# AdaLN block with attention and a mixture of experts: the down product with its operands exchanged, its sum moved to GpSimd, and another order of the three passes

## The reference

```python
h = _layernorm(x) * (1 + ca) + sa
x = x + ga * attention(h)                # 2 query heads of 128, one key and one value head, RoPE, causal
h = _layernorm(x) * (1 + cb) + sb
x = x + gb * ffn(h)

# ffn: 8 experts, all of them on every token, combined with a token's gate w[t, e]
gate = softmax(x @ Wg + bg); thr = sigmoid(x @ Wt + bt) * 0.125
w = (gate - thr) * (gate - thr >= 0);  w = w / sum(w)
h = gelu(x @ W1[e] + b1[e])              # 256 -> 1024
eo = h @ W2[e] + b2[e]                   # 1024 -> 256
out[t] = sum over e of w[t, e] * eo[e, t]
```

## Time and profile before

| | us |
|---|---|
| median of 3 runs | 1946.36 (1943.92 to 1947.73) |
| profiled execution | 1949.09 |
| its span, first to last instruction | 1947.3 |
| PE busy in the span | 1807.6 (93%) |
| DVE, ACT, POOL busy | 1304.9, 1048.1, 756.0 |
| mean granted TensorE clock | 0.968 |

### The profile page before, as it was taken

One profiled execution on the slowest core, in us unless ns is written; L12 is line 12 of the kernel. 1 busy time (PEld: TensorE's weight loads), 2 busy tenths in 40 slices (PEclk: granted clock), 3 DMA queues, 4 the chain that ended last, 5 costly groups with the idle time before them and its releaser, 6 DMA issues.

```text
span 1947.3 us, 32671 instructions
## 1 busy us (share of the span) xinstructions
PE 1807.6 (93%) x11616; PEld 1627.2 (84%) x11616; DVE 1304.9 (67%) x2472; ACT 1048.1 (54%) x2072; POOL 756.0 (39%) x1163
## 2 busy tenths in 40 slices
PE   5789947899589999999999999999999999999997
PEld 4679845798578999999999998888999999999996
DVE  3778747787666666666666666768666666666666
ACT  2567634676454555555555555554555555555553
POOL 4332124333364351615335161739244260624403
PEclk7999968999899999999999999999999999999998
DMA  4000000000000100101010010112110010101002
GB/s 112 26 15 23 18 11 17 23 18 9 31 23 23 33 23 22 42 4 44 11 34 31 14 44 1 33 33 89 53 33 22 23 34 12 44 12 33 12 1 65
DMA packets 56434, 56.04 MB, mean 29 GB/s; under 512 B 8384, under 2 KB 54480, under 8 KB 56272
## 3 DMA queue, kind: packets, MB, share of 16 engines
q1 hardware_dynamic: 56272, 53.95, 9.1%
HBM read 45.55 MB, written 8.39 MB: 28 GB/s over the span
## 4 chain that ended last, share of the span: by engine, by line
PE 62%; issue 5%; DVE 2%; ACT 2%; POOL 1%; POOLq 0%; DVEq 0%; ACTq 0%
PE score_ps L1075 10%; PE score_ps L1076 10%; PE score_ps L1077 9%; PE tr_ps L1110 5%; PE tr_ps L1108 5%; PE tr_ps L1106 5%; PE m_ps L1110 3%; PE m_ps L1108 3%; PE m_ps L1106 3%; PE o_ps L1108 3%; PE o_ps L1110 3%; PE o_ps L1106 3%; DVE h_lo L1276 1%; ACT h_hi L1209 1%; POOL h2f L1437 0%
## 5 line engine op out<-in xcount | busy, mean ns | idle before, releaser
L1205 ACT ACTIVATE g_sb<-c_sb,b_cols 128x512 f32<-128x512 f32 x384 | 276.0, 719 | 439.3 <-DVE c_sb L1340 288.1
L1276 DVE TENSOR_TENSOR h_lo<-g_sb,h_hi 128x512 fp32r<-128x512 f32 x512 | 398.6, 800 | 105.0 <-ACT h_hi L1209 105.0
L1075 PE MATMUL score_ps<-t_hi,w_hi 128*128 128x512 f32 x896 | 361.3, 403 | 27.6 <-ACT p_u L1235 12.2
L1076 PE MATMUL score_ps<-t_lo,w_hi 128*128 128x512 f32 x896 | 355.8, 397 | 0.0
L1077 PE MATMUL score_ps<-t_hi,w_lo 128*128 128x512 f32 x896 | 350.8, 392 | 0.0
L326 POOL TENSOR_TENSOR w_sums<-w_raw 128x128 f32<-128x128 f32 x64 | 42.7, 667 | 664.1 <-PE m_ps L1110 663.3
L1108 PE MATMUL tr_ps<-w_both,h_hi 128*128 128x256 f32 x1024 | 290.6, 284 | 0.0
L1110 PE MATMUL tr_ps<-w_both,h_lo 128*128 128x256 f32 x1024 | 290.5, 284 | 0.0
L1106 PE MATMUL tr_ps<-w_both,h_hi 128*128 128x256 f32 x1024 | 289.3, 283 | 0.0
L1209 ACT ACTIVATE h_hi<-c_sb,b_cols 128x512 fp32r<-128x512 f32 x384 | 271.6, 707 | 0.0
L1075 PEld LDWEIGHTS score_ps<-t_hi,w_hi 128*128 128x128 f32 x896 | 170.9, 191 | 54.5 <-ACT p_u L1235 12.2
(11 more groups left out here) (191 smaller groups left out, 4377.5 us busy)
## 6 DMA issues: line engine op xcount, KB each, us to landing
w_raw<-w_dram SPq DMA_DIRECT2D x128, 256.0 KB, 3.2
x_sb<-x_dram SPq DMA_DIRECT2D x32, 128.0 KB, 2.3
x_scratch<-x_sb SPq DMA_DIRECT2D x32, 128.0 KB, 1.7
t_sums<-x_scratch SPq DMA_DIRECT2D x8, 512.0 KB, 4.6
out_dram<-h2f SPq DMA_DIRECT2D x7, 512.0 KB, 3.2
probs_even<-wmod_dram SPq DMA_DIRECT2D x4, 256.0 KB, 3.9
probs_even<-wmod_dram SPq DMA_DIRECT2D x4, 128.0 KB, 2.3
probs_odd<-wqkvT_dram SPq DMA_DIRECT2D x1, 512.0 KB, 5.8
```

What stands on the lines that cost most here:

```text
L1075: nc.tensor.matmul(bank, hi, t_hi[p][:, b_, :], start=start, stop=False, skip_group_check=True)
L1076: nc.tensor.matmul(bank, hi, t_lo[p][:, b_, :], start=False, stop=False, skip_group_check=True)
L1205: nc.scalar.activation(g_sb[:, m % 2, :], source, ACT.Gelu_apprx_tanh, bias=bias).then_inc(act_g, 1)
L1276: nc.vector.tensor_tensor(h_lo[:, m % 6, :], g_sb[:, m % 2, :], h_hi[:, m % 6, :].bitcast(F32), ALU.subtract).then_inc(dve_lo, 1)
```

## The change

1. `down` exchanges its operands: a 128 x 128 block of W2 is stationary, the hidden values stream, 512 tokens at a time. The result has features on partitions and tokens along the bank. 2 feature halves x 3 passes per block, 24 passes of 512 per group.
2. In `product` and in `down` the passes come in the order low weights x high data, high x high, high weights x low data.
3. The gate is now needed along the free dimension, on all partitions. At the end of each batch's attention SP writes the gates, transposed, to DRAM (16 DMAs), and for each pair of an expert loads 1024 gates to all partitions (`g_rows`). b2 is loaded with features on partitions (`b2_cols`).
4. `evict` replaces `add`: four steps of 128 x 512, `(y + b2) * gate`, into the accumulator for expert 0, into `y_sb` otherwise. POOL then adds `y_sb` to the accumulator, two steps of 128 x 1024 per pair (not for the last pair). All bias work of PE, ACT and POOL goes.
5. The sums are turned back by PE, 16 turns of four 128 x 128 transposes in groups 72 to 79 and 121 to 128, scaled by DVE from PSUM (`scaled`, into `o_sb`) and added to x1 by POOL. The very last pair is turned from `y_sb` after its eviction and added to what the turns of the pair's earlier experts left.
6. `SLOTS` 5 to 4, the ring of `h_hi`, `h_lo` 6 to 5 (`RING`). `cast_tokens` moves ahead of the first GELU of a group, right behind the p_u copy. The low parts of the token sums move from POOL to DVE.

```diff
@@ constants
-SLOTS = 5
+SLOTS = 4
+RING = 5
@@ attention block, sync, after the tiles of batch b
+                    for half in range(NT // GT):
+                        sp.wait_ge(*done(dve_G2, b, "G2", half, 0, G2_STEPS))
+                        for t in range(half * GT, (half + 1) * GT):
+                            sp.dma_start(gT_dram[b, :, t * P:(t + 1) * P].rearrange("e p -> p e"),
+                                         gates[:, b * NT + t, :], allow_slow_non_contiguous=True).then_inc(s_gT[b], 16)
@@ experts, sync
+                    sp.dma_start(b2_cols[:], b2.rearrange("e (k p) -> p e k", p=P), allow_slow_non_contiguous=True).then_inc(l_b2, 16)
+                    def load_gates(r):
+                        b, e, p = parts(r * FS)[0:3]
+                        if e == 0 and p == 0:
+                            sp.wait_ge(s_gT[b], NT * 16)
+                        if r > 0:
+                            sp.wait_ge(dve_evict, r * 4)
+                        sp.dma_start(g_rows[:], gT_dram[b, e, p * 2 * UTOK:(p + 1) * 2 * UTOK].partition_broadcast(
+                            P)).then_inc(l_g, 16)
...
@@ experts, tensor: product
-                        nc.tensor.matmul(bank, hi, t_hi[p][:, b_, :], start=start, stop=False, skip_group_check=True)
-                        nc.tensor.matmul(bank, hi, t_lo[p][:, b_, :], start=False, stop=False, skip_group_check=True)
-                        nc.tensor.matmul(bank, lo, t_hi[p][:, b_, :], start=False, stop=stop,
+                        nc.tensor.matmul(bank, lo, t_hi[p][:, b_, :], start=start, stop=False, skip_group_check=True)
+                        nc.tensor.matmul(bank, hi, t_hi[p][:, b_, :], start=False, stop=False, skip_group_check=True)
+                        nc.tensor.matmul(bank, hi, t_lo[p][:, b_, :], start=False, stop=stop,
                                          skip_group_check=True).then_inc(pe_prod, 1)
@@ experts, tensor: down
-                        for j in range(UNIT):
-                            if first and before >= 0 and j % 2 == 0:
-                                pe.wait_ge(dve_add, before * 8 + u * UNIT + j + 2)
-                            tok = slice(j * P, (j + 1) * P)
-                            nc.tensor.matmul(y_of(u, j), h_hi[:, ring, tok], w2_both[slot][:, f, 0, :], ...)
-                            nc.tensor.matmul(y_of(u, j), h_hi[:, ring, tok], w2_both[slot][:, f, 1, :], ...)
-                            done_ = nc.tensor.matmul(y_of(u, j), h_lo[:, ring, tok], w2_both[slot][:, f, 0, :], ...)
+                        for k in range(KD):
+                            if first and before >= 0:
+                                pe.wait_ge(dve_evict, before * 4 + u * 2 + k + 1)
+                            w_hi, w_lo = (w2_both[slot][:, f, i, k * P:(k + 1) * P] for i in range(2))
+                            o = y_banks[u][k]
+                            nc.tensor.matmul(o, w_lo, h_hi[:, ring, :], start=first, stop=False, skip_group_check=True)
+                            nc.tensor.matmul(o, w_hi, h_hi[:, ring, :], start=False, stop=False, skip_group_check=True)
+                            done_ = nc.tensor.matmul(o, w_hi, h_lo[:, ring, :], start=False, stop=last, ...)
@@ turning back, tensor: a turn stands behind down c21 of groups 72 to 79 and 121 to 128
+                    def turned(source, bank, tiles, made_by):
+                        for i, t in enumerate(tiles):
+                            for k in range(KD):
+                                last = nc.tensor.transpose(bank[:, i * D + k * P:i * D + (k + 1) * P],
+                                                           source[:, k, t * P:(t + 1) * P], ident_sb[:])
+                        last.then_inc(made_by, 1)
@@ experts, vector: evict (half 0 behind c21 of a pair's first group, half 1 behind u2 of its second)
+                        to = acc_of(b, p, u) if e == 0 else y_sb[:, u, :, :]
+                        for k in range(KD):
...
+                            nc.vector.scalar_tensor_tensor(to[:, k, :], y_banks[u][k], b2_cols[:, e, k:k + 1],
+                                                           g_rows[:, u * UTOK:(u + 1) * UTOK], ALU.add,
+                                                           ALU.mult).then_inc(dve_evict, 1)
@@ experts, gpsimd
+                    def add(r):
...
+                        for u in range(2):
+                            acc = acc_of(b, p, u)
+                            pool.wait_ge(dve_evict, r * 4 + u * 2 + 2)
+                            if e > 1:
+                                pool.wait_ge(pool_acc, adds_before(r - PAIRS, u) + 1)
+                            nc.gpsimd.tensor_tensor(acc, acc, y_sb[:, u, :, :], ALU.add).then_inc(pool_acc, 1)
+                    split(2)
+                    split(3)
+                    for n in range(GROUPS + 1):
+                        if n == PARTIAL_FROM:
+                            add((n - 2) // FS)
+                        j, i = divmod(n - 6, PAIRS * FS)
+                        if n >= 6 and i < FS and j * FS + FS + i < B * E * FS:
+                            split(j * FS + FS + i)
+                        for b, p in ((0, 1), (1, 0), (1, 1)):
+                            if n == (b * E * PAIRS + p - 1) * FS:
+                                tokens(b, p)
+                        if n > 1 and n % FS == 1 and n != PARTIAL_FROM:
+                            add((n - 2) // FS)
+                        if n in TURN_AT:
+                            turn(TURN_AT[n])
```

More of the change, by code:

```diff
@@ L973, in adaln_block @@
                 w2_both.append(mx(f"w2_both{i}", [P, 2, 2, D], F32R))
-            h_hi, h_lo = mx("h_hi", [P, 6, UTOK], F32R), mx("h_lo", [P, 6, UTOK], F32R)
+            h_hi, h_lo = mx("h_hi", [P, RING, UTOK], F32R), mx("h_lo", [P, RING, UTOK], F32R)
             g_sb = mx("g_sb", [P, 2, UTOK])
@@ L1048, in _ @@
                         load_weights(sp, q)
+                        if q >= 9 and q % FS == 1:
+                            load_gates((q - 9) // FS * 2 + 2)
                         if q == E * FS + 5:
-                            sp.wait_ge(pool_tlo, 3 * 6)
+                            sp.wait_ge(dve_tlo, 3 * 4)
                             for v in range(2):
                                 load_x1(v)
-                        if q in (E * FS + 7, E * FS + 9):
-                            for v in range(q - E * FS - 7, q - E * FS - 5):
-                                store(v)
-                                load_x1(v + 2)
@@ L1057, in _ @@
-                    for v in range(4, 7):
+                        if q == E * FS + 9:
+                            store_then_load(0)
+                            sp.wait_ge(pe_turn, FS)
+                            for v in (2, 3):
+                                load_x1(v)
+                            store_then_load(1)
+                        if q in (E * FS + 10, E * FS + 11):
+                            store_then_load(q - E * FS - 8)
+                    for r in (LAST - 1, LAST):
+                        load_gates(r)
@@ L1096, in down @@
                         f, u = WHERE[name]
-                        slot, ring = slice_of(n) % SLOTS, made(n, name) % 6
+                        slot, ring = slice_of(n) % SLOTS, made(n, name) % RING
                         first = fs == 0 and name in ("c11", "c22")
@@ L1124, in bias @@
[L1124 to L1135 removed]
+                        for k in range(KD):
[5 more added lines that the diff above has]
+                            nc.tensor.matmul(o, w_hi, h_hi[:, ring, :], start=False, stop=False, skip_group_check=True)
+                            done_ = nc.tensor.matmul(o, w_hi, h_lo[:, ring, :], start=False, stop=last,
+                                                     skip_group_check=True)
+                            if last and k == 0:
+                                done_.then_inc(pe_y, 1)
@@ new lines, in down, with turn @@
+                        done_.then_inc(pe_down, 1)
+                    def turned(source, bank, tiles, made_by):
[4 more added lines that the diff above has]
+                        last.then_inc(made_by, 1)
+                    def turn(n):
+                        k = TURN_AT[n]
+                        b, p, u, half, r = turn_source(k)
+                        pe.wait_ge(dve_u2, min(n + 1, GROUPS))
+                        pe.wait_ge(pool_acc, adds_before(r, u) + 1)
+                        turned(acc_of(b, p, u), bank_b, (2 * half, 2 * half + 1), pe_turn)
@@ L1329, in _ @@
                         if n > 1 and n % FS == 1:
-                            add(n - 2, 1, range(UNIT))
+                            evict(n - 2, 1)
+                        if n % FS != 1:
+                            sum_tokens(n)
                         if ups:
@@ L1345, in _ @@
                         if ends:
-                            add(n - 1, 0, range(3))
+                            evict(n - 1, 0)
+                        if ups and n in TURN_AT:
```

(31 more changed lines are left out.)

299 lines of the change are left out of this document (125 added, 174 removed).

## The result

| | before | after |
|---|---|---|
| median, us | 1947.05 (1943.92 to 1948.28, 4 runs) | 2075.57 (2067.21 to 2078.04, 4 runs) |
| profiled execution, its span | 1949.09, 1947.3 | 2078.04, 2076.3 |
| PE busy | 1807.6 | 1764.4 |
| DMA packets under 512 bytes | 8384 | 44240 |

What follows compares the result with a forecast made beforehand. TensorE's passes were taken to bound steady groups at 10.59 us. Terms -20 - 17 - 18 + 6 + 18 + 3 + 10.5 - 2 = -19.5 gave 1929.6 profiled, 1927 us as median; range 1903 to 1957.

Steps and rivals of the forecast that it cites:

- The gates by DMA: End of each attention batch: SP's 16 single-float stores, 1.4 us per 1024 pieces, delay the next block; +10.5 us, ends +3 and +43.
- rival 3: End of second attention block: single-float DMAs hold SP 3.54 us each, +43 instead of +10.5, 1960 us; chance 0.14.
- Batch 0's are covered ... until SP's next store: Batch 0's gate stores on SP hide behind the first tiles of batch 1, until SP's next store.
- b2_cols lands beside VectorE's own 7 us: Load of b2_cols (2048 floats) lands while VectorE does its own 7 us of token work.
- Down product turned: TensorE's down product: 48 passes of 256 become 24 of 512, a group 10.43 instead of 10.59 us; -20 us.
- New order: TensorE's passes, low weights with high data first: taken as 0, with 38 us more or less possible.
- Additions: GpSimd's expert sums block VectorE's h_lo and stall TensorE, +18 us; groups with a turn on VectorE before L1350, +3.
- Bias off and the other excess: Expert groups: bias work leaves TensorE, -17 us; much of the other 25 us of excess goes too, -18.
- turns: TensorE turning sums back: 16 turns of 4 transposes, 0.35 us a turn, +6 us.
- Tail: After the expert groups: 1.1 us more before the last pass, then eviction, transposes, adds and store; -2 us.

Runs made afterwards that it cites:

- base: Changed kernel with SP's 32 gate stores replaced by two TensorE transposes, a ScalarE copy and one DMA in 512-byte rows: 1905.77 us, 0.9781 of the kernel before.
- the narrow run: Against the changed kernel with gates by transposes: each 512-column pass of the turned down product split into two of 256; 1937.17 us, 0.9944 of the kernel before.
- the additions ahead of the split: Gates by transposes, both additions waiting for all four evictions; then GpSimd's additions moved before the weights' split: 1881.88 us, 0.9658 of the kernel before.
- the late wait: Against the kernel with additions before the weights' split: down product waits for h_lo only before its last two passes; 1880.57 us, 0.9658 of the kernel before.

## Why the prediction was wrong

By its own terms:

- **The gates by DMA, +10.5: the step that failed.** It took 1.4 us per 1024 single floats from the issues behind the cos load, 2048 pieces of 256 bytes, with 3.54 as the upper end. Measured: SP is held 6.0 and 5.8 us a DMA. The prediction named the weak spot itself (rival 3: "cos and sin have 256 bytes a piece, these 4") and then kept the larger piece's price as both value and end, though no row had a piece below 256 bytes: an end far outside belonged there. Loss at the block's border 84 to 86 us, of the forecast 10.5; in all the stores cost 169. (The line on one descriptor per element that the prediction cites stands under "Rules for kernel authors" of the Trainium skill's "DMA: Bandwidth & Descriptors". Transfers under 512 bytes agree with it: 44240 in after, 10976 without the stores.)
- **"Batch 0's are covered ... until SP's next store": right at its own price, wrong at the real one.** Cover ended near 50 us; the series took 96. It cost the rest of the late start, some 60 us (145.0 - 84).
- **"b2_cols lands beside VectorE's own 7 us": right, if nothing stands in the queue.** 2.9 us in base, 35.3 behind the stores; with the weights in the same queue, +24 in group 0. The cost of a series goes on after SP is through with it: batch 1's last store landed 35 us after SP's last issue was done.
- **Down product turned, -20:** -50 by the steady group (10.20, not 10.43), -31 as the narrow run measured it with the additions in place. The 0.2317 of a wide pass was read among narrow ones; beside narrow passes the wide ones are slower too. The row was right, its cause not: it was taken as a property of the pass. (The rule of the Trainium skill, "TensorE: Matmul & The Clock Gate", Part 1, 8 us in all, is further off still.)
- **New order, 0:** shown twice, 0 within 0.1%.
- **Additions, +18 (and +3):** +37. The mechanism and its place are as drawn, to a tenth: addition 2.41, lows 3.00, TensorE idle 0.93. Too small were what follows (passes behind the stall run at 0.23 to 0.34, the second addition costs 0.4 more; 1.67 a time instead of 0.9) and pair 1's (0.66 instead of 0.4). Part of it is the term above: faster passes leave less slack. Beside narrow passes the same additions cost 14 x 1.16 + 13 x 0.06 = 17 us, beside wide ones by the same sum 32.
- **Bias off and the other excess, -35, turns +6:** not measured by a run of their own. What is left of -38.6 when -50 and +37 are taken away is -26, forecast -29. Turns: groups 72 to 79 take 5.3 us over steady ones with the additions gone, so nearer 9 for all.
- **Tail, -2:** -1.4.

The terms after the start sum to -30 forecast, -40 measured. That these are near is luck in part: the passes gave 30 us more than forecast and the additions took 16 more. Rival 3 had the right mechanism, but the wrong price and only one of its places: it named the end of the second attention block (43 us against 84), not batch 0's series (61) nor group 0 (24).

## What to carry to other kernels

Price a DMA by the number and the size of its contiguous pieces until they have landed, not by what its issue costs, and where no row has a piece that small, leave the upper end open or transpose on chip: two TensorE transposes and one DMA replaced 32 stores and 170 us. An issuing engine pays for a slow series three times: the series, the barrier that waits for it, and every load queued behind. GpSimd additions that hold up VectorE are free or dear by which of its steps they fall on; one wait moved them for 20 us. Terms that share a slack don't add up: the additions cost 17 us beside slow passes and 32 beside fast ones. The best kernel here, the change with these two edits and the additions ahead of the split, takes 1881.9 us, 3.4% less than before (1880.6 with the late wait, the same within noise).

## What the runs showed of the hardware

Single-float stores to DRAM, from the first issue to the last landing: 7.8 ns each when one partition's floats land 8 KB apart, 3.4 to 3.8 at 512 bytes; runs of 8 bytes 16 KB apart 3.0 ns each. SP was held for 5.8, 2.4 to 3.2 and hardly any of it. Wide passes (512 columns) among wide ones start 0.227 us apart; among narrow ones 0.231 to 0.233 on average, and for a few passes after a stall 0.23 to 0.34. A shift of the tiles by 64 bytes a partition made a group of 45 passes 10.25 us instead of 10.20. The causes are open.
